# Attention score matmuls: two head parities on separate row halves of the array, maximum pass on 112 rows

## The reference

```
q = rope(x @ Wq.T)   # 2 x 32 heads x 1024 x 16
k, v                 # 2 x 8 heads x 1024 x 16, each serves G = 4 query heads
scores = q @ k.T / sqrt(16), causal mask
ctx = softmax(scores) @ v
```

## Time and profile before

| what | us |
|---|---|
| median of three executions | 1794.19 |
| span of the profiled execution | 1792.7 |
| PE (matmul) busy | 1521.2 (85%) |
| VectorE busy | 1148.1 (64%) |
| ScalarE busy | 607.1 (34%) |
| GpSimd busy | 340.2 (19%) |
| attention, from the first DMA of its own to the last weighted sum | about 1130 to 1719 |

### The profile page before, as it was taken

One profiled execution on the slowest core, in us unless ns is written; L12 is line 12 of the kernel. 1 busy time (PEld: TensorE's weight loads), 2 busy tenths in 40 slices (PEclk: granted clock), 3 DMA queues, 4 the chain that ended last, 5 costly groups with the idle time before them and its releaser, 6 DMA issues. The chain is left out here.

```text
span 1792.7 us, 24031 instructions
## 1 busy us (share of the span) xinstructions
PE 1521.2 (85%) x7034; PEld 1036.6 (58%) x7034; DVE 1148.1 (64%) x2429; ACT 607.1 (34%) x859; POOL 340.2 (19%) x382
## 2 busy tenths in 40 slices
PE   0399889898846881999999999699999999999969
PEld 0366657566535660777777776355555555555447
DVE  5576875768645455455555543688687786888527
ACT  4224223242223330111111111046456465666632
POOL 2243343334312230000000000012122121121211
PEclk9988979889767895999999999579899898999979
DMA  7200000100023432100000000402112111211032
GB/s 263 94 1 1 24 24 1 47 1 24 1 89 125 150 124 89 30 25 18 24 25 18 15 9 0 87 8 48 28 27 54 27 27 27 54 27 29 2 131 82
DMA packets 48596, 84.12 MB, mean 47 GB/s; under 512 B 8899, under 2 KB 16657, under 8 KB 48506
## 3 DMA queue, kind: packets, MB, share of 16 engines
q1 hardware_dynamic: 41874, 78.13, 15.0%
q10 hardware_dynamic: 6632, 4.97, 0.9%
HBM read 58.54 MB, written 24.26 MB: 46 GB/s over the span
## 5 line engine op out<-in xcount | busy, mean ns | idle before, releaser
L1515 ACT ACTIVATE f_prob<-f_bank 128x1024 f32<-128x1024 f32 (+3 forms) x384 | 304.4, 811 | 216.6 <-PE f_bank L1612 214.5
L1594 PE MATMUL f_bank<-f_kst,f_qst 96*128 96x512 f32 (+3 forms) x768 | 282.8, 412 | 24.9 <-DMA f_qst<-q_scr 12.5
L1535 DVE CUSTOM_DVE_ANT_0 f_bank<-f_bank,f_mask 128x128 f32<-128x128 f32 (+3 forms) x512 | 248.5, 503 | 79.5 <-PE f_bank L1594 64.0
L1594 PEld LDWEIGHTS f_bank<-f_kst,f_qst 96*128 96x128 f32 x768 | 153.0, 204 | 181.0 <-DVE f_mx L1535 62.3
L1612 PE MATMUL f_bank<-f_qst,f_kst 98*128 98x512 f32 (+3 forms) x768 | 217.0, 367 | 1.2 <-ACT f_prob L1515 1.2
L1483 POOL TENSOR_SCALAR_AFFINE_SELECT f_prob<-f_prob 128x256 f32<-128x256 f32 x256 | 104.0, 407 | 467.8 <-ACT f_prob L1515 467.2
L1538 DVE TENSOR_REDUCE f_mx_first<-f_bank 128x1 f32<-128x512 f32 x256 | 176.1, 688 | 17.4 <-issue 8.1
L1630 PE MATMUL f_bank<-f_prob,f_vst 128*32 128x512 f32 (+3 forms) x1536 | 169.3, 514 | 1.0 <-ACT f_prob L1515 0.8
L37 PE MATMUL d_bank<-xtl,d_wgh 128*128 (+1 forms) x352 | 143.1, 407 | 8.9 <-DMA d_zz<-z_gu_scr 8.9
L1612 PEld LDWEIGHTS f_bank<-f_qst,f_kst 98*128 98x128 f32 x768 | 135.2, 199 | 20.6 <-ACT f_prob L1515 9.3
L1187 ACT ACTIVATE d_hs<-d_bank 128x512 f32<-128x512 f32 (+1 forms) x44 | 26.3, 598 | 348.8 <-PE d_bank L39 348.8
(11 more groups left out here) (225 smaller groups left out, 2761.6 us busy)
## 6 DMA issues: line engine op xcount, KB each, us to landing
f_qst<-q_scr SPq DMA_DIRECT2D x32, 384.0 KB, 6.1
q_scr<-c_qh SPq DMA_DIRECT2D x32, 256.0 KB
wst<-L_ffn_w SPq DMA_DIRECT2D x6, 1024.0 KB, 6.5
f_kst<-k_scr SPq DMA_DIRECT2D x32, 192.0 KB, 5.2
d_qw<-L_ffn_qweight_gu SPq DMA_DIRECT2D x40, 128.0 KB, 2.6
xall<-L_attn_x SPq DMA_DIRECT2D x2, 2048.0 KB, 16.2
xb<-L_attn_x SPq DMA_DIRECT2D x4, 1024.0 KB, 5.6
x_d<-xb SPq DMA_DIRECT2D x4, 1024.0 KB, 4.3
```

The lines of the kernel that those rows point to most:

```text
L1515: act.activation(prob[:, c // 2 % 2, c % 2 * 2:c % 2 * 2 + 2, lo:], score_bank[c % 2][:, :, lo:], ACT.Exp, scale=D ** -0.5).then_inc(exp_d ...
L1535: dve.tensor_tensor_reduce(sc, sc, mask[:, CH - w:CH], 1.0, LEAST, ALU.add, ALU.max, mx[:, u, h % 2, h // 2, q:q + 1]).then_inc(spare_free, 1)
L1594: pe.matmul(spare[v][:, 0:w], qst[0:M_ROW, u, h // 2, q * P:q * P + P], kst[0:M_ROW, u, h % 2, at:at + w], start=True, stop=True).then_inc ...
```

## The change

The parities move to separate halves of the 128 rows: parity 0 to rows 0 to 47 with its maximum in row 48, parity 1 to rows 64 to 111 with its maximum in row 112. A score matmul now reads only its own parity's 49 rows (0 to 48 or 64 to 112), where it read all 98. An item reads rows 0 to 111, where it read 0 to 95, and row 48 of `qst` has to be zero for it, so `load` gets a fifth DMA that copies zeros into it, and `qk_in` counts five. VectorE clears all of `qst` at the start. The items of the two parities alternate, where the heads came one after the other.

```diff
-M_ROW = 2 * PART
+HALF_ROWS = P // 2
...
-ITEMS = [(h, q, at, min(CH, (q + 1) * P - at)) for h in range(HG) for q in range(QB) for at in range(0, (q + 1) * P, CH)]
+ITEMS = [(2 * i + par, q, at, min(CH, (q + 1) * P - at)) for i in range(HG // 2) for q in range(QB)
+         for at in range(0, (q + 1) * P, CH) for par in range(2)]
+
+
+def stack_rows(par, extra=0):
+
+    return slice(par * HALF_ROWS, par * HALF_ROWS + PART + extra)
+
...
-LOADED = 4 * 16
+LOADED = 5 * 16
+ITEM_ROWS = HALF_ROWS + PART
...
                 for par in range(2):
-                    r = slice(par * PART, par * PART + PART)
+                    r = stack_rows(par)
...
+                sp.dma_start(qst[PART:PART + 1, u].bitcast(F32), kst[P - 1:P, 0].bitcast(F32)).then_inc(qk_in[u], 16)
+
...
                 for par in range(2):
-                    sp.dma_start(qst[M_ROW + par:M_ROW + par + 1, u].rearrange("o i (b q) -> o (i b) q", q=P).bitcast(F32),
+                    row = par * HALF_ROWS + PART
+                    sp.dma_start(qst[row:row + 1, u].rearrange("o i (b q) -> o (i b) q", q=P).bitcast(F32),
...
             for u in range(STACKS):
+                dve.tensor_scalar(qst[:, u], fixed[:, :, :].broadcast_to([P, HG // 2, T]), 0.0, None, ALU.mult)
                 dve.tensor_copy(kst[:, u], fixed[:, :, :].broadcast_to([P, 2, T])).then_inc(cleared, 1)
...
-                pe.matmul(spare[v][:, 0:w], qst[0:M_ROW, u, h // 2, q * P:q * P + P],
-                          kst[0:M_ROW, u, h % 2, at:at + w], start=True, stop=True).then_inc(spare_ps, 1)
+                pe.matmul(spare[v][:, 0:w], qst[0:ITEM_ROWS, u, h // 2, q * P:q * P + P],
+                          kst[0:ITEM_ROWS, u, h % 2, at:at + w], start=True, stop=True).then_inc(spare_ps, 1)
...
                 for hh in range(2):
-                    mm = pe.matmul(score_bank[c % 2][:, hh, lo:], kst[0:M_ROW + 2, u, hh, k * P:k * P + P],
-                                   qst[0:M_ROW + 2, u, c % 2, h * CH + lo:(h + 1) * CH], start=True, stop=True)
+                    r = stack_rows(hh, 1)
+                    mm = pe.matmul(score_bank[c % 2][:, hh, lo:], kst[r, u, hh, k * P:k * P + P],
+                                   qst[r, u, c % 2, h * CH + lo:(h + 1) * CH], start=True, stop=True)
...
     fixed = np.zeros((P, 2, 1), f)
-    fixed[M_ROW, 0], fixed[M_ROW + 1, 1] = -1, -1
+    fixed[PART, 0], fixed[HALF_ROWS + PART, 1] = -1, -1
```

More of the change, by code:

```diff
@@ L1346, in layer1_attention @@
         fixed = sb("fixed", [P, 2, 1])
-        qst = sb("qst", [P, STACKS, 2, T], F32R)
+        qst = sb("qst", [P, STACKS, HG // 2, T], F32R)
         kst = sb("kst", [P, STACKS, 2, T], F32R)
```

## The result

The changed kernel takes 2090.43 us (median of four executions, 2071.37 to 2129.5) against 1793.97 us for the kernel before (four, 1789.52 to 1795.21). The ratio is 1.163, with a 95% interval of 1.156 to 1.169: slower by 296 us (difference of the medians; the ratio is taken without the one execution of 2129.5 us, which lies over 1.5% above the fastest). The forecast was 2198 in a range of 1850 to 2270: the sign and the range held, the time was 108 us too high, and a slowdown of 404 us was forecast where 296 were measured. The profiled execution took 2083.84 us, its span is 2082.1.

The account below looks back on a forecast made before the run. PE was taken to set the pace. At half clock, 15 groups of 60 us plus 13 for branches made 913 instead of 514.4 (+398.6); group 15 +2, start +2, output +1: span 2196.3, median 2198 us, range 1850 to 2270.

Parts of the forecast that it names:

- excursions: Each step's switch from full-row matmuls to half-row scores and back drains the array: 0.37 us full clock, 0.58 half.
- The overlap: A step's two score matmuls run side by side on separate halves, saving 4.2 us a group, 7.7 at half clock.
- the branches: Three loop branches in the attention cost 4.3 us each besides the clock, 13 us together.
- start: Extra clearing by VectorE and the fifth DMA's issue delay the attention's first item by 2 us (1 to 4).
- group 15: The attention's last group, without items, takes some 34 us at half clock instead of 32: +2.
- The mixture: In the attention the full clock is back for about half of the groups: about 2035 us, chance 0.15.
- The likeliest case: Half clock throughout the attention, groups of 60 us: 2198 us, own range 2150 to 2270, chance 0.50.
- rival A: In the attention the clock comes back despite the drains, groups 4.5 us longer: 1871 us, chance 0.18.
- 112 rows and the fifth DMA: Items on 112 rows instead of 96 cost nothing, and the 8 KB DMA is hidden behind loads issued ahead.
- B: Half rows beside full rows cost no switch at the score pairs, a pure gain: 1733 us, chance 0.10.
- C: Score halves pay switches but stream in turn, 7.7 us more a group at half clock: 2313 us, chance 0.03.
- D: Nothing happens at the score pairs, neither overlap nor switch: 1797 us, chance 0.04.

Follow-up runs that it names:

- e2: Changed kernel with both matmuls of each score pair on the same half (parity 0 computed twice, parity 1 left out): 2286.73 us, one execution.
- e11: Changed kernel with the items in the old order, head after head: 2069.06 us.
- e4: Changed kernel with each item reading only its own parity's 48 rows, parities still alternating: 1893.3 us, ratio 1.056 to the kernel before.
- e3: Changed kernel with every item matmul issued twice, 768 matmuls more: 2002.89 us, ratio 1.119 to the kernel before.
- e10: e6 with every item matmul issued twice: 2229.34 us, ratio 1.243 to the kernel before.
- e7: Kernel before with only the new item order, the two parities alternating: 1819.67 us, ratio 1.016.
- e12: Changed kernel with the old item order, items on 112 rows and each score matmul over all 128 rows: 1794.12 us, ratio 0.9993 to the kernel before.
- e8: e6 without the fifth DMA and without the clearing of qst: 1983.23 us.
- e9: Kernel before with one added matmul of 128 columns on rows 0 to 47 ahead of each score pair: 2159.89 us.
- e6: Changed kernel with items on their own parity's 48 rows and in the old order, head after head: 1969.86 us, ratio 1.090 to the kernel before.

## Why the prediction came out as it did

*The direction, right, and for its reason.* 24 excursions a group cost more than 24 saved matmuls (7.4 against 4.2 us at full clock, 15.0 against 7.7 at half). The overlap was put at 7.7 us a group at half clock and measured 8.1 (e2). The price of an excursion was taken whole from matmuls of 2 to 8 rows, 0.37 and 0.58 us. Counted back from the groups it is (35.45 - 32.25 + 4.2) / 24 = 0.31 at full clock (e11) and (60.51 - 53.2 + 7.7) / 24 = 0.62 at half: the choice held for half of the rows, within 0.06 us. The 53.2 in the second is the prediction's sum and no measurement. The group at half clock came out at 60.51 us for a forecast of 60. At full clock 36.8 was forecast; e11 and the order give 37.1, the estimate below 37.6. There two errors nearly cancel, the excursion that was 0.06 too dear (1.5 us a group) and the order of the items that was put at nothing (1.65).

The Trainium skill, "TensorEngine Tiling (Array Packing)", section Key Properties, has the drain at a change of tiling mode and the independence of tiles within one. These traces agree with both: 0.43 us to the load behind a pair that streams for 0.21, and 0.01 us between an item and a score matmul of the other half in e4.

*The clock: the step that failed.* The prediction said that the changed kernel enters the steps at half clock "and I expect it not to leave it before the attention ends". It left it: the clock was full for about 181 of the 797 us. Five of the 15 periods took 40.65 to 41.68 us, 207.05 together, the first 45.36, and the other nine 544.87 together: 797.3. The forecast had 15 x 60 + 13 for the branches = 913. This one term is 116 us too much; start, group 15 and output together are 1.5 too little (5 against 6.5), which gives the 114 us by which the span was missed.

About 100 of the 116 us are the clock's: 93 in the five periods (300 less 207.05), some 6 in the first, little elsewhere. The others are terms of the sum. The first period runs from the maxima that go ahead of step 0 to those of step 19 and holds 20 of a group's 24 steps: 51.26 us against 60.08 in e11, both wholly at half clock, so 9 us that were counted too much. And the branch that the kernel after takes at half clock costs 1.2 us (61.68 against 60.51), not the 4.3 that were read off at full clock.

As to why, the sum compared the mean of a group, 38.4 us of streaming in 59.4, with the stretches in the earlier trace rows, and a group isn't even. The rises of 1413, 1515, 1635, 1799 and 1901 came about 10.5 us behind the maxima's DMAs, at the end of steps 20 to 23, in which scores and weighted sums have 512 columns and six of the eight items 384 or 512. The four that held for 31 us ended about the end of step 19, with items and a weighted sum of 128 columns, many changes of shape and a wait for VectorE. That this is the reason was read and not tried, and it can't be all: the same steps 20 to 23, at half clock and with PE busy for 10.51 of 10.51 us each time, were followed by a rise after 1504.69 and by none after 1444.09. The mixture, which had a chance of 0.15 and 2035 us, was nearer (55 us off, the forecast 108). The likeliest case's own range of 2150 to 2270 missed the result; the stated range held since it reached down to rival A, and that is width, not insight.

*Clock and drains, apart.* A full-clock group of the kernel after can be estimated from a period of 41.68 us: its first 10.6 at half clock do 0.175 of a group, so 31.1 do 0.825, and a whole one takes 37.6. That is 5.35 more than 32.25, 80 us in 15 groups, of which 25 are the order's (1.65 a group). The other 200 or so of the 282.9 are the clock's. That is a sum from rows, and e3 supports it by a run: with all drains kept and more work added, the clock held and 88 us came back.

*The rule on a busy TensorE.* The stretch from 1300 of the kernel after has PE busy for 40.00 of 40.00 us at 0.50, and e10 498 of 500. The Trainium skill, "TensorE: Matmul & The Clock Gate", section "Why this matters for your kernels", asks for a TensorE that is kept busy without long idle gaps. With the clock so kept the time would have been rival A's 1871. Both traces contradict the rule, as the earlier trace rows did.

*"The alternating order changes neither count nor widths": wrong.* Priced at nothing, it costs 1.65 us a group at full clock, 26 us in the kernel before (e7). The name of what hides it was given, VectorE's slack of "9 us at full clock"; but slack over a whole group doesn't cover bunched items; whether the pairs of 512 columns behind three banks or the uneven steps do it stays open. At half clock nearly all is covered (60.08 against 60.51).

*112 rows and the fifth DMA at nothing: right* (e12, and e8 for the group). *The start*, 2 (1 to 4): 2.7 measured up to the first item. *Rivals:* A (the clock comes back) held for 181 of 797 us only; B (faster) needed a change of shape under 0.09 us, and 24 x 0.31 over 47 changes is 0.16; C (no overlap) is refuted by the records and e2; D by the changed group period.

*What stays open.* That fewer rows keep the clock down is shown by e10 beside e3 and e11. That added changes of shape do so for part of the time is shown by e9, less the share of its matmuls on few rows. What the chip weighs, and why the clock falls at the narrow place of a group, was read from the trace and not tried. The executions of one kernel can differ more than usual where the clock swings (58 us in the kernel after, 90 in e9, but 11 in e4 and 4 in e3; 6 before), and nothing here says what decides.

## What to carry to other kernels

Before putting a matmul on part of the rows, count its neighbours: here each excursion from full-row matmuls cost 0.3 us at full and 0.6 at half clock, more than the pair's overlap gave. Where items and scores were given halves alike (e4, e6), that price was mostly gone, but the clock was down, and these versions too were slower than the kernel before. Price every PE edit at both clocks, and read the clock over the stretches of a period, not only at its mean. An order that leaves all counts and widths alone can still cost where another engine has little slack.

## What the runs showed of the hardware that was not expected

Adding 768 matmuls made the changed kernel 88 us faster (e3), since TensorE's clock came back. The number of rows seems to count for the clock: at the same 64,512 columns a group, items on 112 rows brought 1.00 for 132 us (e3), items on 48 rows 0.50 throughout, with fewer drains (e10). With added drains of some tenths of a us, which no record shows as idle time, the clock was at half for 80 us in e9, and full for 120 us at another time. In the kernel after it fell four times with no idle time of PE over 0.9 us. And matmuls of 48 and 49 rows in different halves start 0.01 us apart although they belong to different instructions, operands and lines (e4).
